# Gated cross-attention and a 4-bit FFN on one core: bias columns spread by TensorE, the two chosen sets marked by replacement and weighed by a tanh of all scores, and another order of the set-up calls

## The chip, the cores and the metric

The kernel runs on one core of a Trainium2 chip. The metric is the device time of one execution in microseconds (us), median of several runs. Everything is float32 at the interface. The engines are called by their names in the profile: PE (TensorE; PEld is its weight load), DVE (VectorE), ACT (ScalarE), POOL (GpSimd) and SP (SyncE). SPq, ACTq and POOLq rows are DMA issues and other work of an engine's queue.

## What is computed

`x` is 8 sequences of 256 tokens with 256 features. Two gated residual steps follow each other.

```python
# step 1: routed cross-attention
q      = layernorm(x) @ W_q.T + b_q
scores = (q @ desc_router.T) / 16                     # 64 sets per token
scores = where(token_to_sets names the set, scores, -inf)   # 4 names per token
keep the top 2 scores of each token, softmax over them
x = x + tanh(g_xattn) * (weights @ ctx)               # ctx: 8 x 64 x 256
# step 2: feed-forward, weights of 4 bits with a scale per 32
gate, up = layernorm(x) @ Wg.T, layernorm(x) @ Wu.T   # 2048 wide
inter    = gelu_tanh(gate) * up
x = x + tanh(g_ffn) * (inter @ Wd.T)
```

## The kernel before

**Tiling.** The 8 sequences are taken in four chunks of two (`CB` = 2, `CHUNKS` = 4), 512 tokens to a chunk. The FFN of a chunk runs over 16 units of 128 hidden features: gate product, up product, and, two units later, the down product. Each product is three matmuls over high and low parts of the operands (`w_hi`, `w_lo`, `xt_hi`, `xt_lo`). The 4-bit weights are unpacked in the first chunk alone: ACT compacts bytes (`compact`), DVE makes codes in three stages (`unpack`), POOL multiplies in the scales (`scale_rows_of`, `scale_down_of`, into `w_nat`), PE turns the tiles (`turn_tile`), ACT and DVE write the high and the low part (`rows_high`, `rows_low`, `down_tile_high`, `down_tile_low`). They stay in SBUF for the other chunks.

**Attention of one sequence b.** PE turns x (`turn_x`), ACT copies it (`x_t_out`), PE scores it (`score`). The layer norm's mean is folded into `score_w` by `fold_router`; its variance comes from DVE (`input_stats`, `input_variance`) and POOL's power (`root_1`, out `rstd`). DVE reads the scores with `rstd` and `score_bias` (`read_scores`), finds the top 8 of each token (`find_top`), and subtracts the second from the first (`find_lead`). ACT takes two tanh of 2 columns (`lead_out`), DVE finds the positions (`find_where`: value load and index search, L855, then a comparison with an iota of 256 columns, L863), and weighs them (`weigh`, L877 of 256 columns and L881 of 128). PE turns the result (`turn_probs`), ACT copies it (`probs_out`), PE attends (`attend_first`) into the bank into which it has put x (`add_x`). Statistics of the sum (`update_stats`, `update_variance`), POOL's `root_2`, DVE's `find_shift`, ACT's `normalise`, PE's `turn_normed`, ACT's `ln2_high` and DVE's `ln2_low` end with the operand of the FFN. Sequences 4 to 7 gather their two rows by index instead.

**Bias.** `score_bias` is the bias b_q projected on the 64 sets, plus a mask. b_q is loaded as a row of 256 to 64 partitions. DVE multiplies it by the router (L1023) and sums it (L1025). PE spreads the 64 sums over all partitions (`spread_bias`, L1189). DVE adds the mask (L1039).

**What sets the order.** There is no scheduler: each engine's instructions run in the order in which the block of that engine is written, and semaphores order the engines among each other. In the first 30 us, the order is a list of calls by hand on each of PE, DVE, ACT and POOL; after it a loop over chunks and units. `warm(n)` on PE is n matmuls on zeros into a bank that nobody reads. The first chunk's first two units are special: PE takes the products of the first sequence alone (256 columns) for gate 0, up 0, gate 1, up 1, and then those of the second sequence for the same four; from gate 2 on both sequences are taken together (512 columns).

## Time and profile before

| | us |
|---|---|
| median of 3 runs | 310.67 |
| lowest and highest run | 310.47, 311.12 |
| the profiled execution | 311.26 |
| its span, first to last instruction | 309.5 |
| PE busy in the span | 302.0 (98%) |
| DVE, ACT, POOL busy | 223.6, 155.9, 144.8 |

The page shares the busy time out over the whole span. A stretch table (rows below) gives the same for pieces of it, and a timeline gives the start and the duration of each instruction. Instructions of one engine overlap a little in the pipeline, so that the distance from start to start is the better measure of what one of several in a row costs.

### The profile page before, as it was taken

How to read it: one execution, taken by the hardware profiler on the slowest of the kernel's cores; microseconds unless marked ns; L12 is line 12 of the kernel's file. 1: busy time of each engine (PE TensorE's matmuls, PEld its weight loads, DVE VectorE, ACT ScalarE, POOL GpSimd, SP SyncE). 2: the span in 40 equal slices, each digit the busy share in tenths (PEclk: the TensorE clock that was granted, in tenths of full speed). 3: DMA queues.
4: the chain of work that ended last, by engine and by line, in shares of the span. 5: the costliest groups of instructions: out<-in, count | busy, mean ns of one | idle time of the engine just before them, and what ended most of it. 6: DMA issues, size and time to landing. Idle time of an engine off the chain costs nothing.

```text
span 309.5 us, 4648 instructions
## 1 busy us (share of the span) xinstructions
PE 302.0 (98%) x1537; PEld 251.0 (81%) x1537; DVE 223.6 (72%) x478; ACT 155.9 (50%) x287; POOL 144.8 (47%) x138
## 2 busy tenths in 40 slices
PE   6998999999999999999999999999999999999996
PEld 4777888787788788888888888888888888888885
DVE  3999999899985669687676678777676565544545
ACT  3476665657455453435555453444654533444341
POOL 3447455636742342876353325866442233432421
PEclk9999999999999999999999999999999999999999
DMA  6970440020000021326240111424130001110102
GB/s 184 253 186 0 150 124 0 0 37 1 0 2 0 2 34 17 77 57 123 70 101 3 17 17 26 94 53 85 63 94 0 0 15 26 26 40 0 37 0 68
DMA packets 47288, 16.11 MB, mean 52 GB/s; under 512 B 38944, under 2 KB 44448, under 8 KB 47264
## 3 DMA queue, kind: packets, MB, share of 16 engines
q1 hardware_dynamic: 44576, 12.92, 18.0%
q0 software_dynamic: 864, 2.10, 2.5%
q10 hardware_dynamic: 1824, 0.79, 1.1%
q8 instruction: 12, 0.20, 0.3%
q14 instruction: 12, 0.10, 0.1%
HBM read 11.08 MB, written 3.15 MB: 46 GB/s over the span
## 4 chain that ended last, share of the span: by engine, by line
PE 78%; issue 7%; POOL 6%; DVE 4%; ACT 2%; DMA 2%; SPq 0%; DVEq 0%; POOLq 0%
PE ring_ps L1317 49%; PE acc_ps L1351 17%; PE acc_ps L1364 4%; PE att_ps L1364 3%; POOL act_lo L525 3%; POOL w_nat L507 2%; DMA x_sb<-in_x_dram 2%; PE att_ps L1219 1%; POOL w_nat L518 1%; PE ring_ps L1302 1%; ACT act L695 1%; DVE act L1006 0%; DVE act L1000 0%; DVE x_sb L1157 0%; ACT act L691 0%
## 5 line engine op out<-in xcount | busy, mean ns | idle before, releaser
L525 POOL TENSOR_TENSOR act_lo<-act,act_hi 128x512 fp32r<-128x512 f32 x63 | 82.1, 1302 | 118.8 <-ACT act_hi L702 118.6
L1317 PE MATMUL ring_ps<-xt_hi,w_hi 128*128 128x512 f32 (+1 forms) x264 | 103.8, 394 | 1.0 <-ACT xt_hi L675 0.7
L1317 PE MATMUL ring_ps<-xt_hi,w_lo 128*128 128x512 f32 (+1 forms) x264 | 100.9, 384 | 0.0
L1317 PE MATMUL ring_ps<-xt_lo,w_hi 128*128 128x512 f32 (+1 forms) x264 | 100.2, 384 | 0.0
L691 ACT ACTIVATE act<-ring_ps 128x512 f32<-128x512 f32 x64 | 38.1, 596 | 84.2 <-PE ring_ps L1317 83.8
L1000 DVE SCALAR_TENSOR_TENSOR act<-act,ring_ps 128x512 f32<-128x512 f32 x64 | 43.7, 683 | 39.1 <-ACT act L691 38.9
L1006 DVE SCALAR_TENSOR_TENSOR act<-act,ring_ps 128x512 f32<-128x512 f32 x64 | 43.8, 685 | 27.2 <-ACT act L695 25.9
L1317 PEld LDWEIGHTS ring_ps<-xt_hi,w_hi 128*128 128x128 f32 x264 | 49.7, 188 | 11.1 <-issue 1.2
L1317 PEld LDWEIGHTS ring_ps<-xt_lo,w_hi 128*128 128x128 f32 x264 | 49.0, 188 | 10.3 <-DVE xt_lo L938 0.2
L695 ACT ACTIVATE act<-act 128x512 f32<-128x512 f32 x64 | 40.5, 632 | 32.7 <-DVE act L1000 32.7
L1317 PEld LDWEIGHTS ring_ps<-xt_hi,w_lo 128*128 128x128 f32 x264 | 49.8, 188 | 8.3
L1012 DVE TENSOR_TENSOR act<-act,ring_ps 128x512 f32<-128x512 f32 x63 | 43.3, 687 | 6.3
L702 ACT ACTIVATE act_hi<-act 128x512 fp32r<-128x512 f32 x63 | 39.3, 623 | 4.2 <-DVE act L1012 4.2
L1351 PE MATMUL acc_ps<-act_hi,w_hi 128*128 128x512 f32 x96 | 29.9, 392 | 0.0
L1351 PE MATMUL acc_ps<-act_hi,w_lo 128*128 128x512 f32 x96 | 29.6, 390 | 0.0
L1351 PE MATMUL acc_ps<-act_lo,w_hi 128*128 128x512 f32 x96 | 29.6, 389 | 0.0
L1351 PEld LDWEIGHTS acc_ps<-act_hi,w_lo 128*128 128x128 f32 x96 | 18.0, 188 | 3.9
L1351 PEld LDWEIGHTS acc_ps<-act_lo,w_hi 128*128 128x128 f32 x96 | 18.0, 188 | 3.8
L1351 PEld LDWEIGHTS acc_ps<-act_hi,w_hi 128*128 128x128 f32 x96 | 17.8, 188 | 3.6
L507 POOL TENSOR_TENSOR w_nat<-code_bits,scales_sb 128x512 f32<-128x512 fp8e5 x16 | 16.5, 1054 | 6.2 <-DVE code_bits L974 6.2
L484 POOL TENSOR_TENSOR rstd<-var,minus_half 128x2 f32<-128x2 f32 x8 | 5.6, 698 | 18.4 <-DVE var L827 18.2
L1302 PEld LDWEIGHTS ring_ps<-ident,w_nat 128*128 128x128 f32 x84 | 10.1, 140 | 3.8 <-POOL w_nat L507 1.1
(129 smaller groups left out, 331.9 us busy)
## 6 DMA issues: line engine op xcount, KB each, us to landing
x_t<-in_x_dram SPq DMA_DIRECT2D x48, 32.0 KB, 2.1
w_nat<-w_nat SPq DMA_DIRECT2D x96, 16.0 KB
out_dram<-x_sb SPq DMA_DIRECT2D x6, 256.0 KB, 2.2
x_sb<-in_x_dram SPq DMA_DIRECT2D x1, 1024.0 KB, 8.4
ln_dram<-normed SPq DMA_DIRECT2D x16, 64.0 KB, 2.2
w_nat<-ln_dram SPq DMA_DIRECT2D x16, 64.0 KB, 2.0
packed<-L_ffn_gate_W_packed_dram SPq DMA_DIRECT2D x3, 256.0 KB, 2.9
packed<-n_L_ffn_up_W_packed_dram SPq DMA_DIRECT2D x3, 256.0 KB, 3.3
```

What stands on the lines that cost most here:

```text
L507: pool.tensor_tensor(w_nat[:, r % 2, i * GU:(i + 1) * GU].rearrange("p (b k) -> p b k", k=BLK // 2), codes, s, ALU.mult).then_inc(scaled, 1)
L525: pool.tensor_tensor(act_lo[:, s % RING, :], act[:, s % ACT_RING, :], act_hi[:, s % RING, :].bitcast(F32), ALU.subtract).then_inc(inter_lo, 1)
L691: sc.activation(act[:, s % ACT_RING, :], bank_of("gate", s), ACT.Square).then_inc(squared, 1)
L695: sc.activation(act[:, s % ACT_RING, :], act[:, s % ACT_RING, :], ACT.Tanh, scale=GELU_SCALE * GELU_CUBIC).then_inc(tanh_done, 1)
L702: sc.activation(act_hi[:, s % RING, :], act[:, s % ACT_RING, :], ACT.Copy).then_inc(inter_hi, 1)
L1000: dve.scalar_tensor_tensor(a, a, 1.0 / GELU_CUBIC, bank_of("gate", s), ALU.add, ALU.mult).then_inc(cubic_done, 1)
L1006: dve.scalar_tensor_tensor(a, a, 1.0, bank_of("gate", s), ALU.add, ALU.mult).then_inc(gated, 1)
L1012: dve.tensor_tensor(a, a, bank_of("up", s), ALU.mult).then_inc(inter_done, 1)
L1302: i = pe.transpose(bank_of("tile", k)[:, o * P:(o + 1) * P], w_nat[:, r % 2, at:at + P], ident[:, :])
L1317: i = pe.matmul(into[:, tok], wt[:, n, w], xt[:, c % 2, k, tok], start=(k, j) == order[0], stop=(k, j) == order[-1])
L1351: i = pe.matmul(acc_ps[:, a, :], wt[:, n, GU + a * P:GU + (a + 1) * P], h, start=(n == 0 and part == 0), stop=(n == UNITS - 1 and part == 2))
L1364: ins = pe.matmul(last_sums(i, h), lhs[:, s % RING, t:t + P], wt[:, n, GU:CODES], start=(n == 0 and part == 0), stop=(n == UNITS - 1 and p ...
```

## The change

**Bias.** `b_q` is now loaded as two columns of 128 partitions (`bq_t`, 256 elements of 4 bytes, each on its own), and PE multiplies each column, broadcast over 128, by the turned router, in two matmuls that add up. The two DVE instructions go. `spread_bias` stands behind `turn_router` and ahead of `turn_x(0)`, and waits for that load. The load of the token lists goes from POOL's queue to ACT's, ahead of that of `b_q`.

**Choice.** The scores are half as large as before, and have 6 spare columns of 3e38. `find_lead` makes minus the sum of the two best; a memset puts 3e38 in the six other places of `top8`. ACT takes tanh(2 score - sum) of all 64 columns of both halves, and adds 1 (128 columns). DVE replaces the 8 values in the scores by 2e38 (`match_replace`, 70 columns), and one instruction of 128 columns takes `soft` where the mark stands. Sequences 0 to 3 do this; 4 to 7 are as before with other constants.

**Order.** The lists of calls of DVE, ACT and PE are written in another order. POOL only loses its first DMA and has one memset of 24 columns more.

```diff
-            pool.dma_start(tok_sb[:, :, :], token_sets.rearrange("(p h) k -> p h k", h=HALVES)).then_inc(tokens_loaded, 16)
+            pool.memset(scores[:, :, :, SETS:], SPARE).then_inc(spares_made, 1)
...
-            sc.dma_start(bq_sb[:, :], b_q.rearrange("(a d) -> a d", a=1).to_broadcast([SETS, D])).then_inc(small_loaded, 16)
+            sc.dma_start(tok_sb[:, :, :], token_sets.rearrange("(p h) k -> p h k", h=HALVES)).then_inc(tokens_loaded, 16)
+            sc.dma_start(bq_t[:, :], b_q.rearrange("(k p) -> p k", p=P),
+                         allow_slow_non_contiguous=True).then_inc(small_loaded, 16)
...
             def lead_out(b):
+                for h in range(HALVES):
+                    i = sc.activation(soft[:, q, h, :], scores[:, q, h, 0:SETS], ACT.Tanh, bias=lead[:, q, h:h + 1], scale=2.0)
+                i.then_inc(soft_made, 1)
+                sc.wait_ge(soft_made, b + 1)
+                sc.activation(soft[:, q, :, :], soft[:, q, :, :], ACT.Identity, bias=1.0).then_inc(lead_tanh_ready, 1)
...
             def find_lead(b):
-                dve.tensor_tensor(lead[:, q, :], top8[:, q, :, 1], top8[:, q, :, 0], ALU.subtract).then_inc(lead_ready, 1)
+                dve.scalar_tensor_tensor(lead[:, q, :], top8[:, q, :, 0], -1.0, top8[:, q, :, 1],
+                                         ALU.mult, ALU.subtract).then_inc(lead_ready, 1)
+                mark(("spares", b), dve.memset(top8[:, q, :, 2:8], SPARE))
...
             def find_where(b):
-                    i = dve.max_index(top8_at[:, q, h, :], top8[:, q, h, :], scores[:, q, h, :])
-                mark(("picked", b), dve.tensor_tensor(
-                    picked[:, q], iota_i[:, :].unsqueeze(1).unsqueeze(1).to_broadcast([P, HALVES, 2, SETS]),
-                    top8_at[:, q, :, 0:2].unsqueeze(3).to_broadcast([P, HALVES, 2, SETS]), ALU.is_equal))
+                    i = dve.match_replace(marked[:, h, :], top8[:, q, h, :], scores[:, q, h, :], CHOSEN)
...
             def weigh(b):
-                mark(("weighed", b), dve.scalar_tensor_tensor(
-                    picked[:, q], lead_tanh[:, q].unsqueeze(3).to_broadcast([P, HALVES, 2, SETS]), 1.0, picked[:, q],
-                    ALU.add, ALU.mult))
-                dve.tensor_tensor(probs[:, q, :, :], picked[:, q, :, 0], picked[:, q, :, 1], ALU.add).then_inc(probs_ready, 1)
+                dve.scalar_tensor_tensor(probs[:, q, :, :], marked[:, :, 0:SETS], CHOSEN, soft[:, q, :, :],
+                                         ALU.is_equal, ALU.mult).then_inc(probs_ready, 1)
...
-            dve.tensor_tensor(bq_sb[:, :], bq_sb[:, :], router_sb[:, :], ALU.mult).then_inc(bias_weighed, 1)
-            dve.tensor_reduce(set_bias[:, :], bq_sb[:, :], AXIS.X, ALU.add).then_inc(bias_weighed, 1)
...
             def spread_bias():
-                pe.matmul(acc_ps[:, 0, KT * SETS:(KT + 1) * SETS], set_bias[:, :].to_broadcast([SETS, P]),
-                          ident[0:SETS, 0:SETS], start=True, stop=True).then_inc(bias_done, 1)
+                pe.wait_ge(small_loaded, 16)
+                for e in range(KT):
+                    i = pe.matmul(acc_ps[:, 0, BIAS_AT:BIAS_AT + SETS],
+                                  bq_t[:, e:e + 1].to_broadcast([P, P]), router_t[:, e, :],
+                                  start=(e == 0), stop=(e == KT - 1))
```

**DVE, set-up, between the router's copy and the first sequence's choice.** Names: `out_t` holds b_q before; `act` the hits of the token lists; `choice` holds the picked, marked and weighed sets. Before:

```order
L1023 TENSOR_TENSOR out_t<-out_t,router_sb 64x256
L1025 TENSOR_REDUCE set_bias<-out_t 64x1
L1028 TENSOR_TENSOR act<-tok_sb,iota_i 128x512
L820 BN_STATS stats_1<-x_sb 128x6 x2
...
L820 BN_STATS stats_1<-x_sb 128x6 x2
L835 SCALAR_TENSOR_TENSOR scores<-att_ps,rstd_1,score_bias 128x64 x2
```

After, in the same place:

```order
L1050 TENSOR_TENSOR act<-tok_sb,iota_i 128x512
L839 BN_STATS stats_1<-x_sb 128x6 x2
...
L839 BN_STATS stats_1<-x_sb 128x6 x2
L844 BN_AGGR moments_1<-stats_1 128x2 x2
L846 TENSOR_SCALAR var_1<-moments_1 128x2
L854 SCALAR_TENSOR_TENSOR scores<-att_ps,rstd_1,score_bias 128x64 x2
```

The bias leaves DVE, and sequence 1's variance now stands ahead of sequence 0's scores. Before, it stood behind `weigh(0)`.

**PE, from the attention of sequence 0 to the first products of the FFN.** `choice` is `probs` here, `w_nat` the tiles of weights. Before:

```order
L1247 MATMUL att_ps<-ctx_sb,probs_t 128x256 x2
L1226 MATMUL att_ps<-x_sb,ident 128x512
L1165 MATMUL ring_ps<-act 128x256 x4
L1302 MATMUL ring_ps<-ident,w_nat 128x128 x8
L1165 MATMUL ring_ps<-act 128x256 x4
L1235 MATMUL acc_ps<-ident,choice 64x128 x2
L1269 MATMUL acc_ps<-ident,normed 128x128 x4
L1247 MATMUL att_ps<-ctx_sb,probs_t 128x256 x2
```

After:

```order
L1273 MATMUL att_ps<-ctx_sb,probs_t 128x256 x2
L1189 MATMUL ring_ps<-act 128x256 x4
L1252 MATMUL att_ps<-x_sb,ident 128x512
L1328 MATMUL ring_ps<-ident,w_nat 128x128 x8
L1261 MATMUL acc_ps<-ident,choice 64x128 x2
L1295 MATMUL acc_ps<-ident,normed 128x128 x4
L1273 MATMUL att_ps<-ctx_sb,probs_t 128x256 x2
```

The tiles follow `add_x(1)` at once; four of the eight matmuls on zeros go, and the other four now stand ahead of `add_x(1)`.

**ACT, between the two `probs_out`'s and the second sequence's normalised x.** Before:

```order
L602 ACTIVATE code_bytes<-packed 128x768
L608 ACTIVATE w_hi<-ring_ps 128x512
L667 ACTIVATE normed<-att_ps,shift_2,rstd_2 128x256 x2
L641 ACTIVATE probs_t<-acc_ps,half_gate 64x256
L675 ACTIVATE xt_hi<-acc_ps 128x2x256
L608 ACTIVATE w_hi<-ring_ps 128x512
L649 ACTIVATE x_sb<-att_ps 128x512
L602 ACTIVATE code_bytes<-packed 128x768
L615 ACTIVATE w_hi<-acc_ps 128x2x256
L667 ACTIVATE normed<-att_ps,shift_2,rstd_2 128x256 x2
```

After:

```order
L618 ACTIVATE w_hi<-ring_ps 128x512 x2
L686 ACTIVATE normed<-att_ps,shift_2,rstd_2 128x256 x2
L660 ACTIVATE probs_t<-acc_ps,half_gate 64x256
L694 ACTIVATE xt_hi<-acc_ps 128x2x256
L612 ACTIVATE code_bytes<-packed 128x768 x2
L668 ACTIVATE x_sb<-att_ps 128x512
L625 ACTIVATE w_hi<-acc_ps 128x2x256
L686 ACTIVATE normed<-att_ps,shift_2,rstd_2 128x256 x2
```

Both copies of weight tiles now stand ahead of `normalise(0)`, and the compaction of row 1 stands behind `ln2_high(0)`. In the same stretch, DVE has `input_stats(2)`, which waits for the load of sequences 2 and 3, moved from behind `turn_blocks(2)` to directly behind `weigh(1)`, and its `rows_low(0)` and `rows_low(1)` behind that. PE turns the third tile after gate 0's product instead of after up 0's, turns `normed` of sequence 1 ahead of up 1's product, and scores sequence 2 ahead of the last of the eight half products instead of in the loop behind down 0.

## Rows read from the trace of the kernel before

**Rows 1.** Stretch table: busy time and count of each engine, clock, DMA share, GB/s.

```profile
0.00:10.00 10.00, 7.63 (x51) 5.86 (x52) 5.11 (x16) 3.27 (x6) 4.71 (x14) 1.00 0.81 185
...
150.00:200.00 50.00, 50.00 (x230) 41.67 (x229) 36.04 (x77) 25.49 (x47) 22.02 (x20) 1.00 0.20 46
```

**Rows 2.** Waits of PE from 30 us on: us in total, times, longest.

```profile
PE ring_ps L1302 <- POOL w_nat L518: 0.4, 1, 0.4
```

**Rows 3.** Timeline of DVE: start, duration, engine, line, tiles, [idle before].

```profile
7.36 0.74 DVE L820 BATCH_NORM_STATS2 stats<-x_sb 128x6 f32<-128x256 f32 x2
...
9.29 0.74 DVE L820 BATCH_NORM_STATS2 stats<-x_sb 128x6 f32<-128x256 f32 x2
10.12 0.47 DVE L835 SCALAR_TENSOR_TENSOR scores<-att_ps,rstd,score_bias 128x64 f32<-128x64 f32 x2
...
11.02 0.16 DVE L849 TENSOR_TENSOR lead<-top 128x2 f32<-128x2 f32 x1
...
12.61 0.29 DVE L881 TENSOR_TENSOR choice<-choice 128x128 f32<-128x128 f32 x1
12.82 0.24 DVE L825 BATCH_NORM_AGGREGATE moments<-stats 128x2 f32<-128x6 f32 x2
...
15.23 0.40 DVE L849 TENSOR_TENSOR lead<-top 128x2 f32<-128x2 f32 x1
...
22.62 0.16 DVE L925 SCALAR_TENSOR_TENSOR shift<-moments,rstd 128x2 f32<-128x2 f32 x1 [0.21 <-POOL rstd L491]
...
28.88 0.69 DVE L1006 SCALAR_TENSOR_TENSOR act<-act,ring_ps 128x512 f32<-128x512 f32 x1
```

**Rows 4.** Timeline of ACT and of its DMA issues (ACTq).

```profile
1.21 0.55 ACTq L588 DMA_DIRECT2D out_t<-in_L_xattn_b_q_dram  x1
...
8.52 0.28 ACT L711 ACTIVATE score_w<-acc_ps 128x128 f32<-128x128 f32 x1 [0.24 <-PE acc_ps L1180]
...
17.37 0.60 ACT L608 ACTIVATE w_hi<-ring_ps 128x512 fp32r<-128x512 f32 x1 [0.48 <-PE ring_ps L1302]
17.86 1.01 ACT L667 ACTIVATE normed<-att_ps,shift,rstd 128x256 f32<-128x256 f32 x2
...
23.17 1.02 ACT L667 ACTIVATE normed<-att_ps,shift,rstd 128x256 f32<-128x256 f32 x2
```

**Rows 5.** Timeline of PE.

```profile
6.99 0.66 PE L1205 MATMUL att_ps<-ident,x_sb 128*128 128x128 f32 x4 [1.32 <-DMA x_sb<-in_x_dram]
...
13.93 1.13 PE L1247 MATMUL att_ps<-ctx_sb,probs_t 64*128 64x256 f32 x4
14.99 1.13 PE L1226 MATMUL att_ps<-x_sb,ident 128*128 128x512 f32 x2
15.95 0.60 PE L1165 MATMUL ring_ps<-act 128*128 128x256 bf16 x4
16.68 1.09 PE L1302 MATMUL ring_ps<-ident,w_nat 128*128 128x128 f32 x8
...
25.37 0.38 PE L1317 MATMUL ring_ps<-xt_hi,w_hi 128*128 128x256 f32 x1 [0.69 <-ACT xt_hi L675]
...
29.71 0.47 PE L1317 MATMUL ring_ps<-xt_hi,w_hi 128*128 128x512 f32 x1
...
34.91 1.04 PE L1219 MATMUL att_ps<-score_w,x_t 128*128 128x64 f32 x8
```

**Rows 6.** Timeline of POOL.

```profile
14.56 2.06 POOL L507 TENSOR_TENSOR w_nat<-code_bits,scales_sb 128x512 f32<-128x512 fp8e5 x2 [0.52 <-DVE code_bits L974]
```

**Rows 7.** Timeline of SP's DMA issues.

```profile
11.80 0.47 SPq L361 DMA_DIRECT2D x_sb<-in_x_dram  x1
```

**Rows 8.** DMA issues: tiles, queue, times, KB each, median us from issue to landing.

```profile
x_sb<-in_x_dram SPq DMA_DIRECT2D x1, 512.0 KB, 6.1
...
out_t<-in_L_xattn_b_q_dram ACTq DMA_DIRECT2D x1, 64.0 KB, 4.7
scales_sb<-n_L_ffn_gate_scales_dram ACTq DMA_DIRECT2D x1, 64.0 KB, 6.6
```

148 lines of the change are left out of this document (83 added, 65 removed).

## The prediction

> **What bounds the kernel now.** The profiled execution took 311.26 us with a span of 309.5 us, so 1.76 us lie around the span, and the whole stands 0.59 us above the median of 310.67. I read the stretch table first. From 150 to 200 us PE is busy for 50.00 of 50 us at full granted clock; in the first 10 us it is busy for 7.63 [rows 1]. The waits of PE from 30 us on are next: the largest is one of 0.4 us, for POOL's scaled weights [rows 2]. So nothing that DVE, ACT or POOL save behind about 30 us shortens anything, and the change takes no product away from PE. What can move the end is the time at which PE's unbroken work begins. In the timeline that is gate 2's product at 29.71, the first of 512 columns; before it PE waited 0.69 us at 25.37, for the second sequence's operand [rows 5]. The rest is therefore a race through the first 30 us on four engines, and I read it in the timelines of DVE, ACT and PE [rows 3 to 5], step by step from the landing of x to 29.71. What PE gains at 29.71 it keeps to the end.
>
> **The set-up, to the first scores.** x of sequence 0 lands just ahead of 6.99, where PE turns it [rows 5]. DVE gets to its statistics only at 7.36, since the two bias instructions stand ahead [rows 3]. They go: 0.36 us. The variance of sequence 1 comes in ahead of `read_scores(0)`; its two rows stretch from 12.82 to 13.17, 0.35 us [rows 3]. DVE is thus about level, and no longer waits for PE there. PE loses the bias matmuls and two on zeros between `fold_router` and `score(0)`, and takes four turns of sequence 1 instead. I put `read_scores(0)` at 10.0 against 10.12 [rows 3]: 0.1 us gained, and 0.35 us of DVE work already behind it.
>
> **The choice of the two sets.** Before, from the start of `lead` at 11.02 to the end of `weigh` at 12.90 is 1.88 us [rows 3]. After, the load and replacement on DVE are not last: ACT is. Nothing in the trace has a tanh of 64 columns with a bias from SBUF. The lower bound is a copy of 128 columns with immediates, 0.28 us; the upper one is 0.51 us, half of the 1.01 of two of 256 columns with both operands from SBUF [rows 4]. I take 0.33 for each tanh, with the second starting 0.24 after the first, and 0.39 for the addition of 1, nearer to the lower row because of the widths. With `lead` 0.16, five hand-overs of about 0.05 and 0.29 for the last DVE instruction, as L881 [rows 3], that is 1.6 us; by the bounds 1.4 and 2.0. Gain 0.3, on top of 0.1. `attend_first(0)` ended at 15.06 [rows 5]; after, 14.6.
>
> The Trainium skill ("ScalarE: Activation LUTs", What ACT_TABLE_LOAD costs) has 186 ns plus 0.833 ns a column, and 93 ns more for each pointer operand. By it these three are 0.33, 0.33 and 0.39 us, an estimate from that page; the rows of the copy and of `normalised x` agree with it within 0.02 us.
>
> **To the first product.** `add_x(1)` followed at 14.99 [rows 5]. Now four matmuls on zeros come ahead, 0.45 us by L1165, so it starts at 15.05, no earlier. Behind it the four on zeros go that stood ahead of the tiles: tiles at 16.0 against 16.68 [rows 5]. Their weights are there, because DVE finishes unpacking over 1 us earlier, POOL's two instructions of 2.06 us together started at 14.56 [rows 6] and now start near 13.4. ACT copies the first tile from 16.7 (before 17.37), but now also the second one ahead of `normalise(0)`, 0.48 us more by the distance of 17.37 to 17.86: `normalise(0)` at 17.65 against 17.86 [rows 4]. Only 0.2 us are left there. The products of the first sequence start 0.25 us earlier. Here DVE has one new wait: `input_stats(2)` directly behind `weigh(1)`, near 16.9. Its load is issued at 11.80 and lands 6.1 us later, at 17.9 [rows 7, 8]. Behind it are queued both `rows_low`, for which gate 0 waits, and `ln2_low(0)`. From 17.9 they take 0.66, 0.60 and 0.60 us, so that `ln2_low(0)` starts at 19.8, when its input arrives. The wait costs nothing, with no slack.
>
> **To the second products.** `find_shift(1)` goes from 22.62 to about 22.45 [rows 3]. ACT then began `normalise(1)` at 23.17 only, because the copy of the third tile stood ahead of it and came late [rows 4]. PE now turns that tile one product earlier, so the copy is done by 22.3 and `normalise(1)` starts at 22.5: 0.67 us gained. Second products at 24.7 against 25.37 [rows 5].
>
> **To gate 2.** Before, the last tile was turned by 29.44 and gate 2 waited until 29.71, since `gated(0)` on DVE ended only at 29.57 [rows 3, 5]. In the new order `cubic(0)` no longer stands behind three stages of unpacking; `gated(0)` ends near 28.7. The scores of sequence 2 now come ahead of gate 2, 1.0 us, but are gone at 34.91 [rows 5]; they add nothing. With them gate 2 starts at 24.7 + 4.34 - 0.27 + 1.0 = 29.8, which answers to 29.71 + 1.0 = 30.7 before. **Sum: 0.9 us**, made of 0.25 at the first products, 0.4 more at the second, 0.27 at gate 2. Span 308.6, that execution 310.4, median **309.8 us**.
>
> **Costs at nothing.** The four more ACT instructions of 2.0 us in all for sequences 2 and 3, and some 0.9 us less DVE for each, lie beside PE's full stretch. If DVE's cover failed there, PE's one wait of 0.4 us would grow [rows 2].
>
> **Port between DVE and POOL.** `lead` took 0.16 at 11.02 and 0.40 at 15.23, when POOL ran its scaling from 14.56 to 16.62; 15.63, its end, is where the first of POOL's two ends [rows 3, 6]. The new memset of `top8` and `lead(1)` fall into that stretch. Bounds: nothing, and one POOL instruction, 1.05 us. I take 0.3; even the upper bound ends at `find_shift(0)` near 17.4, still ahead of ACT at 17.65, so it does not enter the sum. The Trainium skill ("SBUF — State Buffer", Who interferes with whom) has the rule: an instruction of DVE with two SBUF inputs locks out, and is locked out by, one of GpSimd that reads SBUF. By that rule, the row agrees, and the `lead` in its new form waits as well.
>
> **Rivals.** (1) **The bias arrives late.** b_q is now 256 pieces of 4 bytes, third on ACT's queue, and `turn_x(0)`, which needs nothing of it, stands behind its wait. Before, the second on that queue was issued at 1.21 and landed 4.7 us later, at 5.9 [rows 4, 8]. The load of b_q is issued near 1.8. By the same time it lands at 6.5, by that of the scales, 1,024 small pieces, 6.6 us, at 8.4 [rows 8]. Each part behind 6.55 delays PE by as much, with some 0.1 of slack at DVE. The point from which the change is slower than before is 7.5; at 8.4 it is +0.9 us: 311.6. For it: small pieces are slow here. Against: only 256, and the queue ahead of them carries 64 KB less. In the middle, 7.0, 310.2. The Trainium skill ("DMA: Bandwidth & Descriptors", Rules for kernel authors) says that a last dimension that is not contiguous becomes one descriptor for each element and should be rearranged; the rival is that rule as a mechanism of this kernel. (2) **The load of sequence 2 is late.** If it lands after 17.9, DVE's queue moves one for one: at 18.6, 0.7 us of the gain go, 310.5. For: DMA queues are full then; against: fewer bytes ahead of it. (3) **The new list brings less:** ACT's three instructions at their upper bound, tiles or `gated(0)` blocked by POOL: half of the gain, 310.3. (4) **The clock falls.** With 19 instead of 23 matmuls on zeros ahead of x and a longer idle stretch, PE could be at 1.2 GHz in the start; by durations on matmuls of 128 columns and the set-up's 2.2 us of PE work I put it at 1 us: 310.8. The granted clock is 1.00 in the first 10 us [rows 1]. (5) **More:** x lands earlier, with less beside it on the queues, and POOL's one wait of 0.4 us [rows 2] goes: 309.3.
>
> **How the numbers follow.** Forecast and what lies within 0.3 us of it: 0.45. Bias late: 0.17, half of it in the middle and half slower than before. Load of sequence 2 late: 0.1. Less: 0.12. Clock: 0.06. More: 0.1. The predicted time is 309.8. 80% lie between 309.2 and 310.9. A measurement of this kernel can tell about 0.2%, 0.6 us, from no change: faster means below 310.05, slower above 311.3. Faster: 0.45 less a fifth, plus 0.1 and parts of (1) to (3), 0.52. Slower: the late half of (1) and a part of (4), 0.13. Same: 0.35.
>
> **What would show it.** In the profile after: PE's bias matmuls without an idle time ahead of `turn_x(0)`, which starts at 7.0; `read_scores(0)` at 10.0; tiles at 16.0; `normalise(0)` at 17.65; DVE idle for about 0.9 us ahead of `input_stats(2)`, and that at 17.9; second products at 24.7; gate 2 at 29.8 with the scores of sequence 2 ahead of it. A `turn_x(0)` at 7.5 or later is rival 1. It would be wrong as a whole if PE had new waits behind 30 us.

## The result and the profile after

The changed kernel took **317.69 us** in the median (six runs, 314.11 to 318.82), the kernel before 310.76 us on the same chip (310.44 to 311.12): ratio 1.019, interval 1.0149 to 1.0223. It is slower by 6.9 us where 0.9 us of gain were forecast, and lies outside the range. Here and below, medians are those of all runs, while ratios and intervals go by the fast runs alone and leave out one of these six and two of the six of a3. The runs scatter over 4.7 us, those of before over 0.7. The profiled execution is the fastest of the six: 314.11 us, span 312.3 us, 2.8 us over that of before.

The set-up on PE in the profile after (timeline: start, duration, engine, line, tiles, idle before), against [rows 5]:

```profile
4.34 1.03 PE L1189 MATMUL ring_ps<-act 128*128 128x256 bf16 x6
7.76 0.73 PE L1213 MATMUL acc_ps<-router_t,bq_t 128*128 128x64 f32 x4 [2.39 <-DMA bq_t<-in_L_xattn_b_q_dram]
8.29 1.06 PE L1231 MATMUL att_ps<-ident,x_sb 128*128 128x128 f32 x4
9.14 1.81 PE L1204 MATMUL acc_ps<-router_t,out_t 128*128 128x64 f32 x8
10.74 1.03 PE L1231 MATMUL att_ps<-ident,x_sb 128*128 128x128 f32 x4
```

PE stands for 2.39 us and waits for b_q; `turn_x(0)` starts at 8.29. Its four matmuls take 1.06 us, where 0.66 stand in [rows 5]. The issue table and the stretch table after, against [rows 8] and [rows 1], say why:

```profile
tok_sb<-in_itok_Sx_dram ACTq DMA_DIRECT2D x1, 4.0 KB, 2.7
bq_t<-in_L_xattn_b_q_dram ACTq DMA_DIRECT2D x1, 1.0 KB, 6.0
```

```profile
7.00:8.00 1.00, 0.24 (x2) 0.24 (x3) 0.30 (x2) 0.00 (x0) 0.72 (x1) 1.00 1.24 258
8.00:9.00 1.00, 1.00 (x8) 1.00 (x8) 0.40 (x2) 0.00 (x0) 0.00 (x0) 0.60 1.39 152
9.00:11.00 2.00, 2.00 (x12) 2.00 (x11) 0.94 (x5) 0.61 (x2) 0.69 (x1) 0.50 1.15 178
11.00:12.00 1.00, 1.00 (x8) 1.00 (x7) 0.00 (x0) 0.45 (x2) 0.00 (x0) 0.69 0.91 224
12.00:20.00 8.00, 7.57 (x46) 4.93 (x45) 6.26 (x33) 4.76 (x15) 3.07 (x4) 1.00 0.91 231
```

1 KB needs 6.0 us, and the token lists, issued just ahead of it, 2.7. The third figure from the end is the granted clock: 1.00 until 8, then 0.50 (1.2 GHz) from 9 to 11. PE had been idle for 2.39 us before it fell. DVE's rows after, against [rows 3], with their idle times:

```profile
8.60 0.29 DVE L1061 SCALAR_TENSOR_TENSOR score_bias<-acc_ps,allowed 128x128 f32<-128x128 f32 x1 [1.30 <-PE acc_ps L1213]
...
12.65 0.47 DVE L854 SCALAR_TENSOR_TENSOR scores<-att_ps,rstd,score_bias 128x64 f32<-128x64 f32 x2 [2.68 <-PE att_ps L1245]
...
13.55 0.16 DVE L873 SCALAR_TENSOR_TENSOR lead<-top 128x2 f32<-128x2 f32 x1
...
14.70 0.29 DVE L907 SCALAR_TENSOR_TENSOR choice<-choice 128x128 f32<-128x128 f32 x1 [0.37 <-ACT choice L652]
```

`read_scores(0)` is at 12.65 instead of 10.0, and from there the new list of calls does what was forecast. PE's timeline at the other end of it:

```profile
30.52 1.05 PE L1245 MATMUL att_ps<-score_w,x_t 128*128 128x64 f32 x8
...
32.18 0.40 PE L1343 MATMUL ring_ps<-xt_hi,w_hi 128*128 128x512 f32 x1
```

From 12.65 to gate 2 at 32.18 are 19.5 us, scores of sequence 2 included; before it was 10.12 to 29.71 and 1.0 more for the scores, 20.6 us [rows 3, 5]. So 2.5 us are lost ahead of `read_scores(0)` and 1.0 regained. 1.5 us remain at gate 2. But the span is 2.8 us longer: more is lost behind 30 us, though the waits of PE there are as small as in [rows 2]:

```profile
PE ring_ps L1328 <- POOL w_nat L526: 0.4, 1, 0.4
PE acc_ps L1387 <- POOL act_lo L533: 0.2, 1, 0.2
```

PE passes the same row 1.1 us later between 190 and 248 us. DVE's timeline shows it there, first after, then before:

```profile
202.75 0.69 DVE L1039 TENSOR_TENSOR act<-act,ring_ps 128x512 f32<-128x512 f32 x1 [0.46 <-DVE act L1033]
203.35 2.71 DVE L919 SCALAR_TENSOR_TENSOR x_sb<-more_rows,row_weights,x_sb 128x256 f32<-128x256 f32 x4
...
216.49 2.71 DVE L919 SCALAR_TENSOR_TENSOR x_sb<-choice,row_weights,x_sb 128x256 f32<-128x256 f32 x4 [0.71 <-DMA choice<-in_ctx_dram,rows_at]
```

```profile
201.28 1.67 DVE L892 SCALAR_TENSOR_TENSOR x_sb<-more_rows,row_weights,x_sb 128x256 f32<-128x256 f32 x4
...
213.77 1.67 DVE L892 SCALAR_TENSOR_TENSOR x_sb<-choice,row_weights,x_sb 128x256 f32<-128x256 f32 x4 [0.57 <-DMA choice<-in_ctx_dram,rows_at]
```

The four additions of context rows take 2.71 instead of 1.67 us, for sequence 6 and again for sequence 7, and an idle time of 0.46 has appeared ahead of an instruction that waits for nothing but its predecessor on DVE. PE "works" through it in the record, so no view of waits shows it. The rest of the 2.8 us, some 0.2, lies between 65 and 110 us: from the first scores of sequence 3 to those of sequence 4 PE's timeline has 44.80 us after and 44.61 before. The run of the choice alone, d2, places it.

So there are four questions: the late bias, the clock, the loss at 200 us, and why the median is 3.6 us above the profiled execution.

### The profile page after: what moved, and what is told of

It is laid out like the page before. It is cut to its first block, busy times and chain, and to the rows that moved or that the text cites. A ratio compares the mean times of both kernels' runs of the same rounds, so it can differ in the third digit from the quotient of the medians.

```text
span 312.3 us, 4628 instructions
## 1 busy us (share of the span) xinstructions
PE 303.6 (97%) x1527; PEld 251.3 (80%) x1527; DVE 221.3 (71%) x472; ACT 158.0 (51%) x291; POOL 143.7 (46%) x138
## 4 chain that ended last, share of the span: by engine, by line
PE 69%; POOL 12%; issue 11%; DVE 3%; ACT 2%; DMA 2%; ACTq 0%; DVEq 0%; POOLq 0%
PE ring_ps L1343 41%; PE acc_ps L1387 14%; POOL act_lo L533 6%; PE acc_ps L1400 4%; PE att_ps L1400 3%; POOL w_nat L515 2%; DMA bq_t<-in_L_xattn_b_q_dram 2%; PE att_ps L1245 1%; POOL w_nat L526 1%; PE ring_ps L1328 1%; POOL choice L544 1%; POOL rstd L499 1%; PE acc_ps L1295 1%; PE att_ps L1231 1%; PE acc_ps L1204 1%
## 5 line engine op out<-in xcount | busy, mean ns | idle before, releaser
L515 POOL TENSOR_TENSOR w_nat<-code_bits,scales_sb 128x512 f32<-128x512 fp8e5 x16 | 16.5, 1053 | 13.7 <-DVE code_bits L1001 13.7
L1387 PEld LDWEIGHTS acc_ps<-act_lo,w_hi 128*128 128x128 f32 x96 | 17.9, 188 | 4.3 <-POOL act_lo L533 0.6
```

Source lines behind the costliest of these rows:

```text
L515: pool.tensor_tensor(w_nat[:, r % 2, i * GU:(i + 1) * GU].rearrange("p (b k) -> p b k", k=BLK // 2), codes, s, ALU.mult).then_inc(scaled, 1)
L1387: i = pe.matmul(acc_ps[:, a, :], wt[:, n, GU + a * P:GU + (a + 1) * P], h, start=(n == 0 and part == 0), stop=(n == UNITS - 1 and part == 2))
```

## Experiments

Each kernel has before beside it on the same chip; medians in us; the interval is at 95%. Many of the expected medians were missed: a1, a2, c1, c3, d1 to d4 and e1 came out 0.6 to 5 us above what the author's own theory gave, e3, f1 and f2 some tenths below. What each run decides is therefore read from its profile and its scatter.

| kernel | median | before | ratio (interval) |
|---|---|---|---|
| a1_bias_behind | 314.46 | 310.71 | 1.0128 (1.0097–1.0159) |
| a2_warm_fill | 313.63 | 310.71 | 1.0102 (1.0089–1.0115) |
| a3_after_again | 315.75 | 310.71 | 1.0123 (1.0077–1.0169) |
| b1_warm_less | 310.70 | 310.71 | 1.0042 (1.0010–1.0074) |
| c1_five_waits | 311.44 | 310.59 | 1.0029 (1.0016–1.0042) |
| c2_more_zeros | 312.37 | 310.59 | 1.0059 (1.0043–1.0076) |
| c3_all_mended | 311.81 | 310.59 | 1.0043 (1.0024–1.0063) |
| c4_old_bias | 310.59 | 310.59 | 1.0002 (0.9992–1.0012) |
| d1_old_bias_numbers | 310.91 | 310.73 | 1.0005 (0.9996–1.0013) |
| d2_choice_alone | 310.87 | 310.73 | 1.0001 (0.9993–1.0010) |
| d3_order_alone | 311.93 | 310.73 | 1.0039 (1.0026–1.0052) |
| d4_bias_alone | 316.83 | 310.73 | 1.0192 (1.0177–1.0208) |
| e1_stats_late | 310.77 | 311.03 | 0.9990 (0.9980–1.0000) |
| e2_bias_filled | 312.64 | 311.03 | 1.0057 (1.0038–1.0077) |
| e3_bias_first | 310.82 | 311.03 | 0.9990 (0.9976–1.0003) |
| f1_clear_best | 309.98 | 310.86 | 0.9973 (0.9961–0.9984) |
| f2_before_clear | 310.43 | 310.86 | 0.9987 (0.9978–0.9996) |
| f3_clear_numbers | 310.42 | 310.86 | 0.9988 (0.9979–0.9997) |

### The bias and the clock, in the changed kernel

**a3_after_again** is the changed kernel once more.

> The changed kernel, nothing altered, timed again beside the three others. Theory L (late bias and clock): PE stands still ahead of the bias matmuls until b_q lands, near 7.7 us, and falls to 1.2 GHz or does not come up for a stretch whose length differs from run to run; the time is 314 to 319 us again and scatters by over 2 us. Theory O (other order, new choice): the loss lies behind the first scores, and the scatter is that of the kernel before, under 1 us.

**a1_bias_behind**, PE's list:

```diff
-            spread_bias()
             turn_x(0)
             fold_router()
             turn_x(1)
+            spread_bias()
```

> The changed kernel with its bias matmuls moved behind both turns of x and the fold, so that PE no longer waits for b_q ahead of them; all else is as changed. Theory L: the first turn of x starts near 6.0, the first scores are read near 9.2 instead of 12.65, gate 2's first product of 512 columns comes near 29 instead of 32.2, and the time is 308.5 to 309.5, with a scatter under 1 us. Theory O: at most 1 us of the loss goes, 313 or more.

**a2_warm_fill**:

```diff
-            warm(6)
+            warm(30)
             spread_bias()
```

> The changed kernel with 30 instead of 6 matmuls on zeros ahead of the bias matmuls, which fill PE's idle time until b_q lands but leave the wait where it is. This tells the delay from the clock. If the clock makes most of the loss: the granted clock stays at 1.00, the first scores are read near 11.0 (b_q at 7.7 plus 3.1), 310.5 to 311.5 and little scatter. If the delay alone makes it: 314 or more as without the filling. Theory O: 314 or more too.

In a1's profile `read_scores(0)` is at 9.97 and gate 2 at 29.80, and the span is still 310.0, 0.5 over before: the loss at 200 us is there in full. That 9.97 meets the forecast is in part luck: PE turned x at 5.61 instead of 7.0, and it was the late bias on DVE that held the scores back. In a2 the bias comes at 7.78, `turn_x(0)` at 8.27, and its four matmuls take 0.61 us: full clock. A gain over a3 isn't shown, since the intervals of the two ratios overlap; what differs is the scatter. a3's profiled run had the bias at 6.88, PE idle for 1.24 us, and no fall of the clock (mean 1.000). So the load lands at another time in each run, and the clock fell with 2.39 us of idle time and not with 1.24. But a1 scatters (311.83 to 315.80) although PE waits for no bias, and a2 does not (313.18 to 314.17). That pointed to the number of matmuls on zeros.

### The late loss, the scatter, and the parts

**b1_warm_less** takes the fewer zeros alone, in the kernel before:

```diff
-            warm(15)
+            warm(13)
             turn_router()
-            warm(8)
+            warm(6)
```

> The kernel before with 13 and 6 instead of 15 and 8 matmuls on zeros ahead of the first turn of x, nothing else. If fewer of them alone let the clock fall or not come up: 312 to 318 and scatter. If it takes the long wait for b_q as well: 310.5 to 311.2, as before.

Seven of twelve runs are those of before (310.30 to 310.71), five lie at 313.46 to 314.67. **c2_more_zeros** is the other side, a1 with `warm(15)` and `warm(8)`:

> The kernel with the bias behind turn_x(1), with 15 and 8 zero-matmuls ahead as in the kernel before instead of 13 and 6. Theory Z (what scatters is the clock, and the two zero-matmuls fewer at both places are one cause of it, as b1's outliers of 314 suggest): the runs draw together at 311.8 to 312.3, median 312.0. Rival W (the wait for the bias is what lets the clock fall, whatever stands ahead): here the bias is behind both turns, so scatter would go away only where turn_x(0) doesn't wait either; times from 311.8 to 315.8 as in a1, median above 313.

Its runs keep to 311.57 to 313.25: the group 3 to 4 us up is gone. What such a run is like, the profiled one of **c1_five_waits** shows. That is a1 with waits that are long fulfilled, which become five more instructions of DVE:

```diff
                     s = c * UNITS + n
+                    if s == 21:
+                        for _ in range(9):
+                            dve.wait_ge(iota_made, 1)
```

> The kernel with the bias behind turn_x(1), and nine calls of a wait that is long fulfilled on DVE at unit 21, about 110 us; they are packed into five further instructions, which brings DVE's instruction numbers behind that point back to those of the kernel before. Theory F (the late loss hangs on the number of an instruction in DVE's stream): in every trace of the changed order inter_of stands idle 0.46 us ahead of it at the 448th instruction (200.4) and again at the 576th (300.3), 128 apart, which none of before does; DVE is then 0.35 us behind POOL, so that the last of the four additions of sequence 6 starts at 202.20, 0.08 behind act_lo on POOL, and takes 1.52 instead of 0.41 us, and what follows is late by 1.1 us. It expects: no such idle time at 200, the four additions 1.67 instead of 2.71 us, 56.75 instead of 57.89 us from the scores of sequence 7 (190) to the first of the last chunk (248), and with it 1.1 us less: span 308.9, 310.7 us. Theory O (the changed order of work or the choice itself puts DVE and POOL into each other's way): no change, 57.9 us for that stretch and 311.8 us at best.

The profiled run took 314.44 us, the other six 310.90 to 311.96. Its PE timeline and stretches:

```profile
4.50 1.46 PE L1192 MATMUL ring_ps<-act 128*128 128x256 bf16 x6
6.11 1.12 PE L1234 MATMUL att_ps<-ident,x_sb 128*128 128x128 f32 x4
7.01 1.81 PE L1207 MATMUL acc_ps<-router_t,out_t 128*128 128x64 f32 x8
...
13.63 2.02 PE L1255 MATMUL att_ps<-x_sb,ident 128*128 128x512 f32 x2
...
17.49 1.13 PE L1276 MATMUL att_ps<-ctx_sb,probs_t 64*128 64x256 f32 x4
```

```profile
3.00:8.00 5.00, 4.74 (x23) 3.32 (x21) 2.90 (x10) 2.19 (x5) 1.88 (x4) 1.00 0.80 204
8.00:14.00 6.00, 6.00 (x29) 6.00 (x29) 2.95 (x17) 2.52 (x7) 0.76 (x2) 1.00 1.09 224
```

Its `turn_x(0)` takes 1.12 us, as in the profile after at half clock, and `add_x(0)` at 13.63 still 2.02, against 1.08 in the profile after at 13.40. Only the rows from 17.49 on have their usual times. The 1.00 of the stretch table is no record of full speed: the first record of the granted clock in this trace begins at 17.14, in all others between 3.8 and 7.0, and the table writes 1.00 where there is none. So PE came to full speed near 17 us, though it stood still for only 0.26 us between 3 and 8. With 13 and 6 matmuls on zeros some runs go this way, with 15 and 8 none of c2, c3, c4, d1, d2, e1, e3, f1 and f3 took over 1.5 us more than its median. That the changed kernel's median stands 3.6 us above its profile fits this, but no profile of it fell in such a run, so it isn't shown.

In c1 the four additions of sequences 6 and 7 are at 1.67 us and the idle time of 0.46 is gone, so the late loss hangs on DVE's instruction stream: in the profile after, that idle time stood at DVE's 448th and 576th instruction (waits for semaphores counted too), 128 apart, and five instructions more moved it away. **c3_all_mended** puts together c2, c1's waits, and `input_stats(1)` and `input_variance(1)` ahead of DVE's wait for the bias.

> All mends together: bias behind turn_x(1), 15 and 8 zero-matmuls, DVE's five further instructions at unit 21, and DVE takes the statistics and the variance of sequence 1 ahead of the wait for the bias instead of behind score_bias (in a1 DVE stood idle from 7.1 to 8.7 ahead of score_bias, and read_scores(0) came at 9.97 though the scores were there at 9.3). Sum from a1's profiled 311.8: less 0.5 for read_scores(0) at 9.4, less 1.1 for the late collision: 310.2, against 310.7 of the kernel before; the scatter gone if theory Z holds. If theory O holds instead of F: 311.3. If the downstream gain of 1.0 us that I read from the first pair of traces is no gain, 311.0 or more.

It has `read_scores(0)` at 10.24, the scores of sequence 2 at 29.41, additions of 1.67 us, and is still 1.2 us above before. The profile has the reason at DVE's statistics of sequence 2:

```profile
19.22 0.76 DVE L839 BATCH_NORM_STATS2 stats<-x_sb 128x6 f32<-128x256 f32 x2 [2.08 <-DMA x_sb<-in_x_dram]
```

DVE waits 2.08 us for x of sequences 2 and 3, and gate 2 comes at 31.07, 20.8 us behind `read_scores(0)` instead of 19.5. **c4_old_bias** therefore takes the bias back (row load, product and sum on DVE, one matmul) and keeps choice and order:

```diff
-            sc.dma_start(bq_t[:, :], b_q.rearrange("(k p) -> p k", p=P), ...)
+            sc.dma_start(bq_sb[:, :], b_q.rearrange("(a d) -> a d", a=1).to_broadcast([SETS, D]))
...
+            dve.tensor_tensor(bq_sb[:, :], bq_sb[:, :], router_sb[:, :], ALU.mult)
+            dve.tensor_reduce(set_bias[:, :], bq_sb[:, :], AXIS.X, ALU.add)
```

> The changed kernel with the bias made as before (a row load of 1 KB pieces, product and sum on DVE, one matmul right behind fold_router, tokens' load on POOL's queue, 15 and 8 zero-matmuls); the choice and the order of the four engines are the changed ones. Theory L (the bias as columns is what costs the set-up): read_scores(0) at 9.9 to 10.1, gate 2 at 29.8 with the scores of sequence 2 done, 0.9 us ahead of before, no scatter; 309.8 us if the stretch from 190 to 248 takes 56.8 us, 311.0 if it takes 57.9 (DVE has 595 instructions here, 597 before and 592 in the changed kernel, so neither is sure). Rival O (the order costs it): at or above 312, with scatter.

All of the loss goes, but no gain is left: 310.59 against 310.59. **d1_old_bias_numbers** gives c4 the DVE numbers of before, by the same fulfilled waits.

> The choice and the order as changed, the bias as before (c4), and two further instructions on DVE at unit 21, so that its instruction numbers behind it are those of the kernel before. In c4 PE was 0.79 us ahead of before at 65 us and 0.60 at 190, and lost it again in sequence 7's four additions, which took 2.71 instead of 1.67 us. Theory F (the number of the instruction): both calls of the additions 1.67 us, nothing lost behind 190, and 0.6 to 0.8 us less than before: 309.9 us where before gives 310.6. Rival T (the additions are slow because DVE stands 0.06 us elsewhere against POOL, whatever the numbers): 2.71 for sequence 7 again and 310.6.

c4's row of `input_stats(2)`, then d1's:

```profile
17.98 0.75 DVE L837 BATCH_NORM_STATS2 stats<-x_sb 128x6 f32<-128x256 f32 x2 [0.95 <-DMA x_sb<-in_x_dram]
```

```profile
18.27 0.75 DVE L837 BATCH_NORM_STATS2 stats<-x_sb 128x6 f32<-128x256 f32 x2 [1.89 <-DMA x_sb<-in_x_dram]
```

d1 reads its scores at 9.40, c4 at 10.15, yet d1 comes to gate 2 later, at 30.12 against 29.82. Both are the start of `input_stats(2)`, at the landing of x for sequences 2 and 3, plus 11.84 to 11.86 us. So are a1 (17.95 and 29.80), a3 (18.40 and 30.26), c3 (19.22 and 31.07) and a2 (19.27 and 31.13). With the wait in this place gate 2 is bound by that load, whatever is gained ahead of it.

The three parts, each alone in the kernel before. **d2_choice_alone**:

```diff
-    (subtract, tanh, products and sum of the two sets' columns)
+    match_replace into choice; two tanh of all scores; identity + 1; one product
```

> The kernel before with the choice alone changed (halved scores, tanh of all, the two sets marked by replacement), the order and the bias as before, DVE's numbers behind unit 21 as before. My step: choice 1.6 instead of 1.88 us from the lead on for each of the sequences 0 and 1. ACT still has compact(0) behind lead_out(0). Theory S (the steps stand in line through the set-up): gate 2 0.3 us earlier, 310.3 us. Rival N (the choice of sequence 0 was covered and what ends last is elsewhere): 310.6, within 0.1.

**d3_order_alone** (all four engines' new lists, choice and bias as before):

> The kernel before with the order of the calls on PE, ACT and DVE alone changed, bias and choice as before, 15 and 8 zero-matmuls. DVE has one instruction more than before (598) ahead of the late sequences, as the order splits its waits elsewhere. If the gain of c4 (0.79 us at 65 us) is the order's: 0.5 to 0.8 us ahead at 65 us, and 309.9 if no addition is caught behind 190, 310.9 if one is. If it is the choice's: nothing ahead at 65 us.

**d4_bias_alone** (b_q as columns, `spread_bias()` ahead of `turn_x(0)`, zeros 15 and 8):

> The kernel before with the bias alone changed: b_q as 256 pieces of 4 bytes on ACT's queue behind the tokens, two matmuls ahead of turn_x(0) as in the change, 15 and 8 zero-matmuls, order and choice as before, DVE's numbers behind unit 21 as before. Theory L: PE waits for bq_t until 7 to 8.4 us, turn_x(0) at 7.6 to 9 instead of 7.0, and TensorE stays at or falls to its lower clock in some of the runs: 0.6 to 2 us more without that, up to 5 with it; median 312 to 314, scattered. Rival O (the order is what the late bias meets badly): within 0.5 of before.

d2 gained 0.23 us from `read_scores(0)` to gate 2, forecast was 0.3, and nothing in the median. It gives the gain back further on: from the first scores of sequence 3 to those of sequence 4 it takes 44.79 us, as c4 (44.81) and after (44.80) do, and d3, with the old choice, 44.64, as before does (44.61). So the 0.2 us between 65 and 110 us belong to the new choice of sequences 2 and 3. d3 costs 1.2 us in the median. In its profile PE waits 0.74 us for the choice, and the clock is down for a while:

```profile
12.99 0.41 PE L1237 MATMUL acc_ps<-ident,choice 128*64 128x128 f32 x2 [0.74 <-DVE choice L881]
```

```profile
20.00:30.00 10.00, 10.00 (x68) 9.30 (x66) 7.44 (x22) 6.66 (x13) 4.46 (x5) 0.83 0.27 79
```

But its gate 2, at 30.98, is only 0.3 us late, and this was the slowest of its five runs. At the scores of sequence 5 it is 0.4 us late. Most of the loss in this profile is the one of 200 us again, in another place: 1.2 us between the scores of sequences 5 (124) and 6 (179).

```profile
134.21 0.69 DVE L1012 TENSOR_TENSOR act<-act,ring_ps 128x512 f32<-128x512 f32 x1 [0.46 <-DVE act L1006]
134.82 2.71 DVE L892 SCALAR_TENSOR_TENSOR x_sb<-more_rows,row_weights,x_sb 128x256 f32<-128x256 f32 x4
```

The idle time stands at DVE's 320th instruction, 128 ahead of the 448th, and the additions of sequences 4 and 5 take 2.71 us each. So d3 does not show that the new order needs the new choice. d4 alone costs 6.1 us; its PE timeline and stretches:

```profile
7.40 1.12 PE L1189 MATMUL acc_ps<-router_t,bq_t 128*128 128x64 f32 x4 [1.92 <-DMA bq_t<-in_L_xattn_b_q_dram]
8.31 1.06 PE L1207 MATMUL att_ps<-ident,x_sb 128*128 128x128 f32 x4
```

```profile
6.50:7.50 1.00, 0.10 (x1) 0.10 (x1) 0.52 (x2) 0.00 (x0) 0.90 (x2) 0.84 1.17 324
7.50:16.50 9.00, 8.97 (x36) 7.32 (x37) 3.69 (x18) 2.68 (x8) 0.11 (x1) 0.50 1.08 253
16.50:18.00 1.50, 1.50 (x11) 1.41 (x10) 1.20 (x4) 0.00 (x0) 0.78 (x2) 0.69 1.08 177
```

After 1.92 us without work PE is at half clock from 7.5 to 16.5, and its set-up matmuls take up to twice their time: `turn_x(0)` 1.06 us here and 0.60 in e2, the eight of `score(0)` 1.94 and 1.01 before.

### Clock, queue and load apart

**e2_bias_filled** fills d4's idle time:

```diff
-            warm(8)
+            warm(24)
             spread_bias()
```

> d4 (bias alone changed, matmuls ahead of turn_x(0)) with 24 zero-matmuls instead of 8 ahead of it, so that PE isn't idle from 5.4 to 7.4. Theory K (the clock is the larger part): the granted clock stays at 1.00, turn_x(0) comes at 8.0 to 8.5 instead of 7.0, and the median is 311.7 to 312.5 and no longer scattered, so 4 to 5 of the 6 us were the clock. Rival D (the wait itself costs it, the clock little): 315 or more.

The clock stays at 1.00 and 4.5 of the 6.1 us go, each against its own before; some of that is b_q, which landed 1.0 us sooner behind its issue in e2's profile than in d4's. Of the remaining 1.6 us the profile places 0.8 to 0.9 in the delay itself: `turn_x(0)` at 7.87 against 6.99, gate 2 at 30.55 against 29.71 [rows 5], and a span of 310.3 against 309.5. The other 0.8 is no time of the kernel's, but comes from which executions were profiled: that of before lay 0.6 us above its median and that of e2 0.5 below, and before's median is 0.4 higher on e2's chip. **e3_bias_first** asks whether 256 pieces of 4 bytes are slow in themselves: c3, with the load of b_q first on ACT's queue and `input_stats(2)` behind `turn_blocks(2)`.

> c3 (bias as columns behind turn_x(1), all mends) with the load of b_q as the first on ACT's queue, ahead of w_q and the tokens, and input_stats(2) behind turn_blocks(2) as in e1. If the late landing (5.5 to 6.4 us from its issue) is its place in the queue: bq_t lands by 5, w_q 0.5 later. If 256 pieces of 4 bytes are slow by themselves: bq_t still lands 5 us behind its issue, and w_q with it. Time, from c3's 311.8 less 0.5: 311.3 either way, since the bias isn't waited for behind turn_x(1); under 310.7 only if x(1), which lands at 7.5 to 8.4 in all kernels with columns, lands earlier too.

The issue rows, e3, then c2, where it stands behind the 256 KB of W_q and the tokens:

```profile
bq_t<-in_L_xattn_b_q_dram ACTq DMA_DIRECT2D x1, 1.0 KB, 2.1
```

```profile
bq_t<-in_L_xattn_b_q_dram ACTq DMA_DIRECT2D x1, 1.0 KB, 5.8
```

Same pieces, 2.1 against 5.8 us. So the form alone is not slow; first on the queue it is quick. What makes the third place slow isn't separated: the 256 KB ahead in the same queue, or the loads of x that run beside it. The tokens, behind the same 256 KB, landed in 2.7 to 3.4 us, which speaks against the first as the whole cause. Loaded first and used behind `turn_x(1)`, columns cost nothing that can be measured: 310.82 against 311.03. **e1_stats_late** is d1 with `input_stats(2)` behind `turn_blocks(2)` again.

> d1 (choice and order as changed, bias as before, DVE's late numbers as before) with input_stats(2) back behind turn_blocks(2), where the kernel before has it. Theory X (the landing of sequence 2's input at 18.0 to 18.3 sets gate 2): in d1 DVE stood 1.89 us ahead of input_stats(2) with w_lo and xt_lo queued behind it, and gate 2 came 20.7 us behind read_scores(0) instead of 19.7 as in c4, where it stood 0.95 us. Without that wait gate 2 comes 19.3 to 19.7 us behind read_scores(0) wherever that falls: 29.0 to 29.8, span 308.2 to 308.9, median 310.1 against 310.7 of before. Rival G (something else of the order holds it at the same place, PE's products or the tiles): gate 2 at 29.8 to 30.1 again and 310.7 to 310.9.

DVE no longer waits there (gate 2 at 29.93, 19.94 us behind `read_scores(0)`), but PE waits 0.40 us for `ln2_low(1)` at 25.63: the gain is about 0.1%, with no change still inside the interval.

### The additions at 200 us

Groups of 2.71 to 2.75 us also stand in profiles without such an idle time ahead of them: one each in c4, d4 and e1 (sequence 7) and in d1 and e3 (sequence 5). So it is not the instruction numbers alone. One instruction of the four is the long one: it is caught, as we call it from here on. c4 and before, the additions of sequence 7 as a group (count, then shortest, median and longest duration in ns):

```profile
L917 DVE SCALAR_TENSOR_TENSOR x_sb<-choice,row_weights,x_sb x4: 479/482/1516, 213.2 to 214.4; 128x256 f32<-128x256 f32 x4
```

```profile
L892 DVE SCALAR_TENSOR_TENSOR x_sb<-choice,row_weights,x_sb x4: 479/479/485, 213.8 to 215.0; 128x256 f32<-128x256 f32 x4
```

And POOL's `act_lo` in c4 and in before:

```profile
214.36 1.29 POOL L533 TENSOR_TENSOR act_lo<-act,act_hi 128x512 fp32r<-128x512 f32 x1 [2.16 <-ACT act_hi L719]
```

```profile
214.98 1.62 POOL L525 TENSOR_TENSOR act_lo<-act,act_hi 128x512 fp32r<-128x512 f32 x1 [2.17 <-ACT act_hi L702]
```

The last addition starts 1.19 us after the first: 214.41 in c4, 0.05 behind `act_lo`, and takes 1.52 us; in before 214.96, 0.02 ahead of `act_lo` at 214.98, and takes 0.48, and `act_lo` pays with 1.62. The same holds in d2 and in d1's sequence 7 (0.03 and 0.08 ahead, free), and in d3's sequence 7 and a1's sequence 6 (0.06 and 0.08 behind, caught). The Trainium skill ("SBUF — State Buffer", Who interferes with whom) has it that a DVE instruction with two SBUF inputs and a GpSimd one that reads SBUF lock each other out; the row agrees. To take the collision away, POOL's `act_lo` of these units waits until the third addition is done:

```diff
+                        for b in next_sequences(*divmod(s - 1, UNITS), ADD):
+                            if b >= BY_ROWS:
+                                pool.wait_ge(attn, {4: 63, 5: 72, 6: 93, 7: 102}[b])
                         low_part(s - 1)
```

**f2_before_clear** is the kernel before with this alone (other counts). **f1_clear_best** is e3 with it, `input_stats(2)` behind `ln2_low(1)`, and without the fulfilled waits; **f3_clear_numbers** is f1 with them.

> The kernel before with nothing changed but that same wait on POOL ahead of four of its act_lo. Theory P: all additions 1.67 us; the median equal or up to 0.1 us lower, since before is caught in some runs only, and its highest runs (to 311.6) go. If act_lo is late for PE by that wait: 0.1 to 0.3 us more.

> e3 (b_q loaded first, bias as columns behind turn_x(1), the choice and the order as changed, 15 and 8 zeros) with input_stats(2) behind ln2_low(1), without the further instructions on DVE, and with POOL's act_lo of the unit of the additions held until the third addition has ended. Theory P (the fourth addition is caught by act_lo where it begins after it): all four calls of the additions 1.67 us, though DVE stands idle 0.46 us at its 448th instruction again; gate 2 at 29.4 to 29.8, 310.2 to 310.5 against 310.7 of before. Rival T (what is slow is something else, the rows or the gathers): at least one call of 2.71 us as before, 311 or more.

> f1 with the further instructions on DVE at unit 21. If the idle time at the 448th instruction costs only by what it collides with: the same as f1 within 0.1. If it costs by itself: 0.3 us less than f1.

All additions are at 1.67 us in all three. f1:

```profile
212.31 1.67 DVE L924 SCALAR_TENSOR_TENSOR x_sb<-choice,row_weights,x_sb 128x256 f32<-128x256 f32 x4 [0.50 <-DMA choice<-in_ctx_dram,rows_at]
```

```profile
213.67 1.47 POOL L533 TENSOR_TENSOR act_lo<-act,act_hi 128x512 fp32r<-128x512 f32 x1 [2.24 <-DVE x_sb L924]
```

f2 is 0.43 us faster than before, which in its profile escapes by 0.02 us; that it is caught in some other runs fits, but was not seen. **f1 beats both kernels: 309.98 us**, 0.27% (0.16 to 0.39%) below before. About half of that is POOL's wait, which gives f2 0.43 us without any part of the change. Its `turn_x(0)` is at 5.79, `read_scores(0)` at 9.07, gate 2 at 28.89. f3, with the fulfilled waits, takes the same 118.6 us from the first scores of sequence 7 to the end as f1. It is 0.4 us slower in the median, but the intervals of the two overlap, and the two profiles differ only ahead of 10 us, where no waits were added.

f1 also shows where the idle time went without extra instructions. It has one instruction less ahead of the additions, so that its 448th is a wait for a semaphore; this begins 0.39 us after the one before it, where 0.04 is usual, while the TENSOR_TENSOR at 199.28 still runs for 0.69 us. The delay is there, behind running work, and the additions start at 199.89 as if it were not.

## Why the prediction was wrong

**Wrong: the bias, rival 1.** "PE's bias matmuls without an idle time" failed. The rival gave 6.5 to 8.4 us for the landing and 7.5 as the point of slower; b_q came at 7.7 in the profile after. The failed step is the choice of 6.5, by the 4.7 us that the row load of 64 KB had needed as second on the queue. As third, and in pieces of 4 bytes, b_q needed 4.6 to 6.4 us in nine profiles, and as first 2.1 to 2.2 (e3, f1, f3). A second step failed with it: rival 1 priced the delay one for one. By its own sum a landing at 7.7 gives 1.2 us of delay less 0.9 of gain, 311.0 us; the profile after lost 2.5 us ahead of the scores, and d4 6.1 us in all. The chance of 0.17 was too low: PE's list had been given a wait ahead of everything with no slack. Rival 5 was half right beside it: where PE doesn't wait for the bias first, `turn_x(0)` starts at 5.5 to 6.4 in the seven profiles with columns, and at 6.0 to 7.0 in the eight with the row load, 0.5 us later in the mean. The 6.99 that the prediction built on is the latest of the eight. In the changed kernel the wait for the bias hid that. The Trainium skill ("DMA: Bandwidth & Descriptors", Rules for kernel authors) speaks against the form of the load. By it the layout would be at fault; e3's 2.1 us say that the layout alone was cheap here.

**Wrong: the clock, rival 4.** It was given 0.06 and 1 us, by 2.2 us of PE work at half speed, as a cause by itself. In fact it follows from rival 1: the clock stayed up through idle times of 1.24 to 1.46 us (a3, before, c2) and was down after 1.92 and 2.39 us (d4, after). In d4 it stayed down for over 9 us, and the term measured about 4.5 us (d4 against e2, each against its own before). The other half of rival 4, two matmuls on zeros fewer at each place, was right in direction; some runs then lose 3 to 4 us (b1, c1), which the prediction's 1 us did not cover. The 1.00 that the prediction read for the first 10 us [rows 1] could not have shown it: the clock record of before begins at 4.29.

**Right: the list from `read_scores(0)` on.** Gain 1.0 in the profile after, 0.9 in c4, against 0.9 forecast. Of the choice alone 0.2 instead of 0.3 arrives at gate 2 (d2), although from the start of `lead` to the end of `weigh` it takes 1.44 us in the profile after, less than the 1.6 forecast. The term for tanh was right within its bounds: two tanh end 0.59 us after the start of the first, and the addition of 1 takes 0.31. "`add_x(1)` no earlier" and POOL's early scaling held. a1 met 10.0 and 29.8 as 9.97 and 29.80, with two errors that cancel at the first (x early, bias late) and with the load of x as what sets the second.

**Wrong by 0.2 us: "Costs at nothing".** The new choice of sequences 2 and 3 was put beside PE's full stretch at no price. Between the first scores of sequences 3 and 4 the profiles with it show 44.76 to 45.00 us, those with the old choice 44.60 to 44.66, and this takes back d2's gain.

**Half right: the wait for x of sequence 2.** "Costs nothing, with no slack" held at 17.9. But it is a floor: d1 reads its scores 0.75 us ahead of c4 and gives it back there, and c3 loses about 1.3 us there. Rival 2 described this as a late load; it is an early DVE.

**Wrong: "What PE gains at 29.71 it keeps to the end".** The wait table was read as saying that nothing behind 30 us could lengthen. It shows the waits in one alignment of DVE and POOL, with a margin of 0.02 us between the fourth addition and `act_lo`. Any shift by some hundredths of a microsecond ahead decides over 0.2 us for one catch (from the scores of sequence 7 to the end, 118.6 us in before and 118.8 in c4), and 1.1 us for the catches of sequences 6 and 7 with the idle time on DVE (119.7 in the profile after). Of the 0.9 us that c4 had at gate 2, its profile has 0.6 left at the scores of sequence 7 and, after one catch, 0.4 at the end. In the medians nothing is left, since the profiled execution of before was one of its slower ones.

**Added up**, for the profile after: 2.5 lost ahead of the scores (late bias and clock), 1.0 gained, 1.1 at 200 us, 0.2 by the choice of sequences 2 and 3: 2.8 us. For the median 3.6 us more, which fit the late rise to full speed but were seen in no profile of this kernel. The last 0.5 of the 6.9 us is the profiled execution of before, which lay that much above its median.

**Open:** what the idle time of 0.46 us at the 192nd, 320th, 448th or 576th DVE instruction is, and why it does not appear at each of them (before's 448th has none); only its tie to the number is shown. Open too are what makes b_q slow in the third place, why fewer matmuls on zeros let PE rise late in some runs alone, and f1 against f3.

## What to carry to other kernels

Ask of every transfer that PE waits for what is ahead of it in its queue and what runs beside it, and put the smallest and most urgent first; in d4 a `turn_x(0)` that came 1.3 us late cost 6.1 us, most of it by the clock. When a kernel waits for a load, move work that needs nothing of it ahead of the wait, or fill the idle time with matmuls on zeros. A full engine does not guarantee that a gain at its start reaches the end: look for pairs of DVE and POOL instructions that share SBUF inputs and start within a few hundredths of a microsecond, and fix their order by a wait.
